# Scaling edge weights in PSUM ahead of use, and a six-group ring of gathered rows, in a four-layer graph network

## What is computed

```python
h = silu(edge_attr_10 @ W_fc1 / sqrt(10))          # 100 hidden units for each edge
w1, w2, w3, w4 = split(h @ W_fc2 / sqrt(100), 4)   # 4 x 32 weights for each edge
x0s, x1s = y0[src], y1[src]                        # gathered row: 32 scalars, 32 vectors of 3
ea0, ea1 = edge_attr_4[:, :1], edge_attr_4[:, 1:]
mid0a = w1 * x0s * ea0
mid0b = w4 * dot(x1s, ea1) / sqrt(3)
mid1a = (w2 * x0s)[:, :, None] * ea1[:, None, :]
mid1b = w3[:, :, None] * x1s * ea0[:, None, :]
agg   = segment_sum(concat(mid0a, mid0b, mid1a, mid1b), dst)
```

## Time and profile before

| | us |
|---|---|
| device time, median of 3 runs | 4927.12 (4906.59 to 4927.83) |
| span of the profiled execution, first to last instruction | 4361.2 |
| outside the span, against that median | 565.9 |
| tensor pass in the profile, first gather to last addition | 117 to 1278 |

### The profile page before, as it was taken

How to read it: one execution, slowest core, us unless ns; L and a number is a source line. 1 busy time by engine, 2 the same in 40 slices (tenths; PEclk the granted TensorE clock), 3 DMA queues, 4 the chain that set the end, 5 groups by cost and what they waited for, 6 DMA issues and landing times. The chain is left out here.

```text
span 4361.2 us, 67130 instructions
## 1 busy us (share of the span) xinstructions
PE 3150.7 (72%) x22048; PEld 2138.5 (49%) x22049; DVE 2326.6 (53%) x7490; ACT 1273.1 (29%) x2767; POOL 2831.6 (65%) x2851
## 2 busy tenths in 40 slices
PE   2677777777677888764534457987888688886886
PEld 1666665666555555432322244555555455554444
DVE  5677777777655666666657772335232432324223
ACT  1334344444434444434332240003111121112112
POOL 2777776666534767546747756764777577774775
PEclk8899999999988998975555568998999899997998
DMA  5324455667963444304444558764888578885876
GB/s 181 85 68 96 76 97 91 90 101 102 119 125 88 121 117 116 93 22 85 80 93 79 99 102 266 243 205 156 266 265 262 168 247 263 262 265 168 263 242 181
DMA packets 470576, 659.32 MB, mean 151 GB/s; under 512 B 108665, under 2 KB 335266, under 8 KB 469462
## 3 DMA queue, kind: packets, MB, share of 16 engines
q1 hardware_dynamic: 356438, 377.29, 34.7%
q0 software_dynamic: 113792, 277.69, 24.2%
HBM read 542.27 MB, written 112.46 MB: 150 GB/s over the span
## 5 line engine op out<-in xcount | busy, mean ns | idle before, releaser
L1716 POOL DMA_INDIRECT pass_rows<-table_sage,src_idx x1136 | 1087.0, 957 | 366.7 <-issue 336.7
L1154 POOL DMA_INDIRECT pass_rows<-table_tensor,src_idx x784 | 797.0, 1017 | 350.6 <-issue 223.9
L1775 PE MATMUL pass_dense_ps<-x 128*128 128x512 f16 x2352 | 544.9, 384 | 28.9 <-DMA x<-table_sage 27.9
L2653 POOL DMA_INDIRECT sort_rows<-table_sort,slot_idx x392 | 398.1, 1016 | 183.4 <-issue 118.6
L1382 POOL DMA_INDIRECT pass_rows<-table_gate,src_idx x338 | 331.7, 981 | 174.5 <-issue 96.6
L1775 PE MATMUL pass_dense_ps<-rb 128*128 128x512 f16 x2058 | 424.2, 361 | 25.9 <-DMA rb<-table_sage 24.3
L1837 DVE TENSOR_TENSOR pass_scaled_sums<-pass_sums_ps,rc 128x54 f32<-128x54 f32 (+18 forms) x340 | 60.7, 220 | 577.9 <-PE pass_sums_ps L1800 540.7
L1775 PEld LDWEIGHTS pass_dense_ps<-x 128*128 128x128 bf16 x2352 | 220.7, 99 | 275.7 <-DMA x<-table_sage 28.7
L2567 PE MATMUL pass_counts_ps<-rc 128*128 128x512 bf16 (+13 forms) x1064 | 239.8, 344 | 149.0 <-ACT re L2600 100.5
L1800 PE MATMUL pass_sums_ps<-pass_hot,pass_rows 128*128 128x68 bf16 (+18 forms) x5472 | 214.3, 193 | 162.8 <-DMA pass_rows<-table_sage,src_idx 151.2
L1233 PE MATMUL pass_sums_ps<-pass_hot,pass_prod_a 128*128 128x128 f32 x1568 | 236.4, 298 | 120.0 <-DVE ra L1248 96.7
(11 more groups left out here) (379 smaller groups left out, 6108.9 us busy)
## 6 DMA issues: line engine op xcount, KB each, us to landing
rb<-dense SPq DMA_DIRECT2D x98, 512.0 KB
x<-dense SPq DMA_DIRECT2D x196, 256.0 KB
x<-table_sage SPq DMA_DIRECT2D x196, 192.0 KB
dense<-re SPq DMA_DIRECT2D x11, 3136.0 KB, 26.1
rb<-dense SPq DMA_DIRECT2D x98, 296.0 KB
pass_counts<-dense SPq DMA_DIRECT2D x98, 256.0 KB
rb<-table_sage SPq DMA_DIRECT2D x196, 96.0 KB
table_sage<-x SPq DMA_DIRECT2D x24, 768.0 KB
```

Source lines behind the costliest of these rows:

```text
L1154: nc.gpsimd.indirect_dma_start(rows[:, h, t, :], None, table, bass.IndirectOffsetOnAxis(ap=idx[:, at:at + 1], axis=0)).then_inc(gathered[h ...
L1716: nc.gpsimd.indirect_dma_start(rows[:, h, t, :], None, table, bass.IndirectOffsetOnAxis(ap=idx[:, at:at + 1], axis=0)).then_inc(gathered[h ...
L1775: ins = nc.tensor.matmul(dense_ps[:, a * most_cols + at:a * most_cols + to], table_ring[:, k, from_table:from_table + P], counts_ring[:, k ...
L2653: nc.gpsimd.indirect_dma_start(rows[:, b, j, :], None, table, bass.IndirectOffsetOnAxis(ap=slot_idx[:, at:at + 1], axis=0)).then_inc(gathe ...
```

## The change

ACT no longer multiplies the gathered rows by ea0. It multiplies, in place in PSUM, the two of four weight channels that need ea0 (w1 and w3, 64 of 128 columns for each tile), one group ahead of DVE. DVE then uses the gathered rows themselves in place of `y_ea0`, and where it waited for `weight_made` it waits for `weighed`; its wait for `ea0_made` is gone, as is ACT's wait for `gathered`. ACT's order becomes silu(q+2), four scalings of group q+1, evictions of group q. Before it was silu(q+1), four scalings of group q, evictions of group q. The ring of rows has six slots instead of four, in the room that `y_ea0` took. The wait of ACT for `split_stored` now comes ahead of its first silu.

```diff
+ROW_SLOTS = 6
-        rows = s.sb("rows", [P, RING, GROUP_TILES, width])
+        rows = s.sb("rows", [P, ROW_SLOTS, GROUP_TILES, width])
-        y_ea0, y_ea1 = s.sb("y_ea0", [P, 2, GROUP_TILES, P]), s.sb("y_ea1", [P, GROUP_TILES, 3, MUL])
+        y_ea1 = s.sb("y_ea1", [P, GROUP_TILES, 3, MUL])
 # POOL
-                h = q % RING
-                if holds_back(q - RING + 1):
-                    pool.wait_ge(summed, q - RING + 1)
+                h = q % ROW_SLOTS
+                if q >= ROW_SLOTS:
+                    pool.wait_ge(summed, q - ROW_SLOTS + 1)
 # ACT
-            silu(0, 0)
-            def body(i):
-                for h in range(RING):
-                    q, r = i * RING + h, h % 2
-                    silu(q + 1, (h + 1) % 2)
-                    if holds_back(q - 1):
-                        act.wait_ge(operands_made, q - 1)
-                    act.wait_ge(gathered[h], gathers.count(h, GROUP_TILES * (i + 1)))
-                    for t in range(GROUP_TILES):
-                        ins = nc.scalar.activation(y_ea0[:, r, t, :], rows[:, h, t, :], ACT.Copy,
-                                                   scale=cols(extra["edge_attr"], (q * GROUP_TILES + t) * 4, 1))
-                    ins.then_inc(ea0_made, 1)
-                    for t in build.turns(q, BUILD_TURNS):
-                        for w in build.ended(t):
-                            build.evict(act, w)
+            def weigh(q):
+                act.wait_ge(weight_made, q + 1)
+                for t in range(GROUP_TILES):
+                    scaled = weight_ps[:, q % 2, t * P:(t + 1) * P].rearrange("p (c u) -> p c u", u=MUL)[:, 0:4:2, :]
+                    ins = nc.scalar.activation(scaled, scaled, ACT.Copy,
+                                               scale=cols(extra["edge_attr"], (q * GROUP_TILES + t) * 4, 1))
+                ins.then_inc(weighed, 1)
             act.wait_ge(extra["split_stored"], 16 * SPLIT)
-            for i in range(ITERS):
-                body(i)
+            silu(0)
+            silu(1)
+            weigh(0)
+            for q in range(GROUPS):
+                silu(q + LOOK)
+                if q + 1 < GROUPS:
+                    weigh(q + 1)
+                for t in build.turns(q, BUILD_TURNS):
+                    for w in build.ended(t):
+                        build.evict(act, w)
 # DVE
-                m = TensorMath(nc, GROUP_TILES, weight_ps[:, r, :], rows[:, h, :, :], y_ea0[:, r, :, :],
+                m = TensorMath(nc, GROUP_TILES, weight_ps[:, r, :], rows[:, slot, :, :], rows[:, slot, :, :],
-                dve.wait_ge(gathered[h], gathers.count(h, GROUP_TILES * (i + 1)))
+                dve.wait_ge(gathered[slot], gathers.count(slot, GROUP_TILES * (q // ROW_SLOTS + 1)))
-                dve.wait_ge(weight_made, q + 1)
+                dve.wait_ge(weighed, q + 1)
-                dve.wait_ge(ea0_made, q + 1)
```

More of the change, by code:

```diff
@@ L1111, in tensor_pass @@
             extra["room"].rearrange("p (r t f) -> p r t f", r=2, t=GROUP_TILES)
-        ea0_made, step, dotted, emptied = s.sem("ea0_made"), s.sem("step"), s.sem("dotted"), s.sem("hot_emptied")
+        weighed, step, dotted, emptied = s.sem("weighed"), s.sem("step"), s.sem("dotted"), s.sem("hot_emptied")
         hidden_ps, weight_ps = s.ps("hidden", [P, 512]), s.ps("weight", [P, 2, 512])
@@ L1165, in _, with silu @@
         def _(act):
-            def silu(q, r):
-                if holds_back(q - 1):
+            def silu(q):
+                if q >= 2:
                     act.wait_ge(weight_made, q - 1)
                 act.wait_ge(hidden_summed, q + 1)
-                nc.scalar.activation(hidden[:, r, :], hidden_ps[0:HID, :], ACT.Silu,
+                nc.scalar.activation(hidden[:, q % 2, :], hidden_ps[0:HID, :], ACT.Silu,
                                      scale=1.0 / math.sqrt(BASIS)).then_inc(hidden_made, 1)
-            silu(0, 0)
-            def body(i):
-                for h in range(RING):
-                    q, r = i * RING + h, h % 2
-                    silu(q + 1, (h + 1) % 2)
-                    if holds_back(q - 1):
-                        act.wait_ge(operands_made, q - 1)
-                    act.wait_ge(gathered[h], gathers.count(h, GROUP_TILES * (i + 1)))
-                    for t in range(GROUP_TILES):
-                        ins = nc.scalar.activation(y_ea0[:, r, t, :], rows[:, h, t, :], ACT.Copy,
-                                                   scale=cols(extra["edge_attr"], (q * GROUP_TILES + t) * 4, 1))
-                    ins.then_inc(ea0_made, 1)
-                    for t in build.turns(q, BUILD_TURNS):
-                        for w in build.ended(t):
-                            build.evict(act, w)
-            act.wait_ge(extra["split_stored"], 16 * SPLIT)
-            for i in range(ITERS):
-                body(i)
+            def weigh(q):
[5 more added lines that the diff above has]
+                ins.then_inc(weighed, 1)
+            act.wait_ge(extra["split_stored"], 16 * SPLIT)
+            silu(0)
[8 more added lines that the diff above has]
+                        build.evict(act, w)
         @block.tensor
@@ L1251, in operands @@
                 q, r = i * RING + h, h % 2
+                slot = q % ROW_SLOTS
                 if holds_back(q - 1):
@@ L1298, in _ @@
             dve.wait_ge(added, GROUPS * n_acc)
-    gathers.end_phase([GROUP_TILES * ITERS] * RING)
+    gathers.end_phase([GROUP_TILES * len(range(k, GROUPS, ROW_SLOTS)) for k in range(ROW_SLOTS)])
 def gate_pass(nc, gathers, name, table, idx, rel, iota_half, bases, dense, agg, extra):
```

## The result

Seven runs of the changed kernel have a median of 4937.83 us (4930.30 to 4963.67), seven of the kernel before beside them 4906.59. The ratio is 1.0066, 95% interval 1.0045 to 1.0087: about 32 us slower, where 55 us faster was forecast. A second set (e4), on a chip where before has a median of 4961.52, gave 1.0093 (1.0071 to 1.0115).

What follows compares the result with a forecast made beforehand. It took POOL's gathers to bound the pass early, PE with its evictions from about 600 us, and late rows to break this; -55 - 3 + 17 - 5 - 10, with halves -55.5, gave 4927 - 55 = 4872, range 4833 to 4940.

Steps and rivals of the forecast that it cites:

- The base: Start of the sum: span 4361.2 us, 566 more outside it untouched, so the span's change is added to the median 4927.
- rival 2: Gathered rows in the ring land no sooner with more slots, so only B and C are left: 4940; chance 0.08.
- A: Six ring slots cover DVE's waits for gathered rows from group time 600 us on: -55 us (-28 to -73).
- The tail's -3: At 1259 us the node attributes' load holds the last gathers; six slots cover that: -3 us (0 to -4).
- B: On ACT, mid-group evictions queue behind silu(q+2) and four scalings: 38 groups x 0.45 us, +17 (+15 to +54).
- The rivals' 17.5: Cost of late evictions on ACT, as entered in the sums of rival 2 and of the POOL-floor rival.
- C: silu(q+2) on ACT runs ahead of evictions, so PE's weights wait less for hidden units: -5 us (0 to -12).
- D: TensorE's clock: eight fewer long stops of PE for rows keep matmuls fast: -10 us (0 to -20).
- rival 3: Each mid-group stop of PE grows and pulls the clock down: +103 against -73, 4957; chance 0.12.

Runs made afterwards that it cites:

- e4: The changed kernel as it is, measured again on the chip of three further runs; 1.0093 of before.
- e10: Kernel before with only the ring changed to six slots (16-bit y_ea0, old ACT order), second run; 0.9999 of before.
- e5: Changed kernel with ACT's old order (silu(q+1), scalings and evictions of group q), scaling in PSUM and six slots kept; 1.0008 of before.
- e9: Changed kernel with ACT's old order and a ring of four slots, scaling in PSUM kept; 0.9987 of before.
- e1: Kernel before with only the ring changed to six slots (16-bit y_ea0, old ACT order), first run; 0.9974 of before.
- e8: Changed kernel with evictions parted: mid-group windows ahead of silu(q+2) and the scalings, last-tile windows behind them; 1.0000 of before.
- e12: Changed kernel with eight scalings a group instead of four, all ahead of the mid-group evictions; 1.0145 of before.
- e3: Changed kernel with evictions of group q moved right after silu(q+2), ahead of the scalings of group q+1; 1.0002 of before.
- e13: Changed kernel with eight scalings a group instead of four, mid-group evictions ahead of silu(q+2) and all scalings; 0.9996 of before.
- second profile: The kernel before, unchanged, profiled once more on the chip of the first experiments; 4932.64 us.

## Why the prediction was wrong

**The base.** The step that failed first is "the median of the runs, 4927, has 566 more outside it". Those 566 us are inside the timed spans. All the rows then described an execution in which PE's results reached the waiting engines at once, and POOL or a late transfer could be what set the pace. In the timed one POOL has 11 of 100 us to spare where it was to have none, and taking the waits for rows away gave no time. That the measured 4937.83 lies near rival 2's 4940 is luck: the runs of before beside it have 4906.59 and not 4927, so the change is +32, where that rival had +13.

**A, -55.** The waits for rows do go (41.9 to 5.7), but the time doesn't follow: the step that failed is that a wait of DVE counts in full. There were 41.9 us of such waits in the whole timed pass, where the term took 55 out of 59.3 from 600 on. And none of the 36 that went came back as time: e10 against before, 0.9999; e5 against e9, 1.0008 with six slots and 0.9987 with four; the 0.9974 of e1 was not repeated. Rival 2 had no gain either, but because rows would land no sooner; DVE's waits say that they are there in time. What is as late instead was not found. The tail's -3 is too small to be seen.

**B, +17.** Right in kind, and the term that decides, but mis-sized in price and in count. The window itself was well read where PE's results reach ACT without delay. The four scalings take 0.90 against 0.88 forecast, and in the window above the eviction starts 1.76 after `hidden` starts, against 1.86 forecast and 1.44 in e8. But these are the cheapest windows. Over all 69, eviction follows `hidden` by 2.70 us in the mean before and by 3.64 after: 0.94 later and not 0.45. After, 31 of them take more than 3 us (before 22), and in every one of the 31 silu had itself started over 1.5 us after its hidden layer began, with the scalings and the eviction queued behind it. The count failed too. I took the 38 groups from 89 on (39 by the plan, with 89 itself), as POOL would set the pace ahead of them. PE's stops grew by 65 us, 21 of them in the 20 windows ahead of group 89 and 44 in the 49 others. The two sets measured 32 us and 0.0093 x 4961 = 46 in time, about twice the term and less than the stops. For the four further scalings of e12 the simple product holds better: 69 x 0.42 = 29, where the stops grew by 26 and the time by 32 (1.0145 less the mean of 1.0066 and 1.0093). The rivals' 17.5 is a slip for 38 x 0.45 = 17.1.

**C, -5.** PE's waits for silu fell by 50 us, ten times the term. No run shows that any of it is kept: e8 has two thirds of that gain (85 to 52) and the time of before.

**D, -10.** The other way round. No long stop for rows is saved that PE would have noticed, and the granted clock is lower: 0.89 to 0.87, 0.86 in e4, 0.84 in e12. Little of the 32 us can be laid on it. From 390 to 1370 PE was busy with the pass's own matmuls (sums, weights, hidden layer) for 4.02 us a group after and 4.07 in e4, against 4.03 before and 4.07 in e3, which has the time of before. In e12 it was 4.14 against 3.98 in e13; there slower matmuls are a part of the price. These are single traces.

**The rivals.** The sign is that of rival 3, and its time over the median of before, 4957 / 4927 = 1.006, is close to the 1.0066 measured. Of its mechanism the longer stops in mid-group are what e8, e12 and e13 show; that the clock behind them costs as much again shows in none of them. Its sum was not right: it set +103 against gains of 73, and the runs show no gains and a cost of 32 to 46, so its near hit is luck. I gave it 0.12 because the rows of the quick execution were divided on whether short stops cost clock.

**What no run tells.** None of the kernels is clearly faster than before, so there is no better version to offer. PE's waits can't simply be added up: those for evictions and silu together are 276 us before, 324 after, but 313 in e8, which has the time of before. What holds the pass in its place when these waits shift is open. So is why e8, with 35 us more of PE's stops in mid-group than before, loses nothing.

## To carry over

Hold the profile's span against the time before reading anything else; if they differ by more than a few us, the profile is of another kind of execution, and its waits are not those that the timed kernel has. When steps are put in order on an engine, ask for each which other engine stands for it at that moment: put that one first, and what is needed a group later behind it, even if the engine then idles. A buffer that takes one engine's wait away need not gain time: here the wait went and the time stayed.

## What was new about the hardware

In the timed executions PE's results reach other engines late by its own record. Timeline of before, second profile: a hidden layer and the silu whose wait it ended,

```profile
249.59 0.38 PE L1202 MATMUL pass_hidden_ps<-pass_edge_terms,fc_stack 90*100 90x512 bf16 x1
...
251.44 0.60 ACT L1171 ACTIVATE pass_hidden<-pass_hidden_ps 100x512 f32<-100x512 f32 x1 [4.29 <-PE pass_hidden_ps L1202]
```

and such a pair in the first profile:

```profile
243.56 0.38 PE L1202 MATMUL pass_hidden_ps<-pass_edge_terms,fc_stack 90*100 90x512 bf16 x1
...
244.04 0.60 ACT L1171 ACTIVATE pass_hidden<-pass_hidden_ps 100x512 f32<-100x512 f32 x1 [0.28 <-PE pass_hidden_ps L1202]
```

1.47 us from the matmul's recorded end to silu, against 0.10. ACT stood idle ahead of 76 silus of the pass; these started 1.09 us after the recorded end of their hidden layer in the median, and nine of them over 4.6 us after it. In the first profile it was 0.10 in the median of 51 such places, and 0.38 at most. The Trainium skill, page "Perfetto Trace Analysis", section "Tensor Engine Instruction (MATMUL, LD_WEIGHTS)", says that the end of a matmul in a profile is estimated from its size and not observed; the second profile, with its 1.09 us, agrees, and a matmul's record there is no proof that its result was ready. What makes the two kinds of execution differ was not found.

In-place scaling of 64 columns in PSUM, four in a row, took 0.90 us, and four more directly behind them put the next step off by 0.42.
